# Three small attentions, each in two parts of 256 tokens and in units of 8 heads

## The reference, cut to what matters

```python
x = x + xattn0(ln(x), ctx)       # "0x": 16 heads of 16, biases
x = x + attn0(ln(x))             # "0a": keys and values from a latent of 64
x = x + moe0(ln(x))              # 32 experts, top 4, and one shared expert
x = x + xattn1(ln(x), ctx)       # keys of all 1601 context rows, one head of k and v
x = x + ln(h + attn1(h)) * gamma + beta    # "1a", h = ln(x); causal
x = x + ffn1(ln(x))              # 8 experts, the best one per token
```

## Time and profile before

| | us |
|---|---|
| median of 3 runs (lowest, highest) | 622.85 (621.93, 626.32) |
| the profiled execution | 627.66 |
| its span | 625.7 |
| 0x, 0a and the context, to `up(0)` | 0 to 143.6 |
| moe0 and xattn1 | 143.6 to 441.0 |
| 1a and the last norm, to the last gate's logits | 441.0 to 507.2 |
| the last stage | 507.2 to 625.7 |

### The profile page before, as it was taken

How to read it: one execution, slowest core, us unless ns; L and a number is a source line. 1 busy time by engine, 2 the same in 40 slices (tenths; PEclk the granted TensorE clock), 3 DMA queues, 4 the chain that set the end, 5 groups by cost and what they waited for, 6 DMA issues and landing times.

```text
span 625.7 us, 15065 instructions
## 1 busy us (share of the span) xinstructions
PE 546.8 (87%) x6480; PEld 366.6 (59%) x6480; DVE 326.8 (52%) x648; ACT 290.5 (46%) x467; POOL 111.6 (18%) x192
## 2 busy tenths in 40 slices
PE   4968758887999999789999999999797977999991
PEld 1536524553566666435677677675356544999990
DVE  2235124735566666567999989892465550011111
ACT  1434417523565666348887878787043010332220
POOL 4321141310333333350000000000300002000002
PEclk9978779998999999989999999999898888999997
DMA  8833370001455555440000000000700004388712
GB/s 321 316 129 126 138 260 1 2 15 52 130 157 154 154 151 151 158 179 3 4 3 4 2 4 4 3 3 3 270 2 2 0 2 151 117 295 288 275 35 92
DMA packets 35041, 65.01 MB, mean 104 GB/s; under 512 B 3264, under 2 KB 24640, under 8 KB 34592
## 3 DMA queue, kind: packets, MB, share of 16 engines
q1 hardware_dynamic: 31952, 59.16, 28.5%
q10 hardware_dynamic: 2640, 3.85, 1.8%
q0 software_dynamic: 384, 1.05, 0.5%
HBM read 60.05 MB, written 4.00 MB: 102 GB/s over the span
## 4 chain that ended last, share of the span: by engine, by line
PE 56%; issue 17%; DVE 11%; another core or an unknown queue 7%; DMA 4%; POOL 2%; ACT 2%; SPq 0%; POOLq 0%; ACTq 0%; DVEq 0%
PE ps L1189 9%; PE ps L1298 8%; PE ps L1266 7%; PE ps L1047 7%; PE ps L1211 7%; PE ps L1312 6%; PE ps L996 2%; DMA attn_weights<-in_wall 2%; PE ps L1092 1%; DVE region L887 1%; DVE region L765 1%; DVE region L762 1%; PE ps L1136 1%; DMA const_bf<-in_cb 1%
## 5 line engine op out<-in xcount | busy, mean ns | idle before, releaser
L887 DVE TENSOR_REDUCE region<-ps 128x1 f32<-128x512 f32 x192 | 124.1, 687 | 19.6 <-PE ps L1266 19.6
L665 ACT ACTIVATE region<-ps 128x1024 f32<-128x1024 f32 (+1 forms) x112 | 105.9, 963 | 19.7 <-PE ps L1298 19.2
L1266 PE MATMUL ps<-ctx_kT,region 96*32 96x512 bf16 x768 | 82.0, 383 | 2.6 <-DVE region L887 1.8
L1298 PE MATMUL ps<-region,ctx_kT 98*32 98x512 bf16 x832 | 72.5, 381 | 0.6 <-ACT region L643 0.4
L996 PE MATMUL ps<-const_bf 128*128 128x512 bf16 x226 | 58.5, 420 | 14.7 <-DMA const_bf<-in_cb 8.5
L1312 PE MATMUL ps<-region,ctx_v 128*32 128x128 f32 (+1 forms) x1664 | 70.1, 272 | 0.0
L1189 PE MATMUL ps<-region 128*128 128x512 f16 x264 | 63.7, 386 | 0.1
L1312 PEld LDWEIGHTS ps<-region,ctx_v 128*32 128x32 f32 (+1 forms) x1664 | 56.7, 109 | 9.5 <-issue 0.3
L694 ACT ACTIVATE region<-ps,ctx_v 128x128 f32<-128x128 f32 x88 | 25.1, 368 | 73.1 <-PE ps L1047 73.1
L438 POOL TENSOR_TENSOR region<-region 128x512 f32<-128x512 f32 x33 | 38.2, 1157 | 79.3 <-ACT region L608 77.8
L1211 PE MATMUL ps<-region 128*128 128x256 bf16 x396 | 48.6, 273 | 2.1 <-DVE region L839 2.1
(11 more groups left out here) (216 smaller groups left out, 762.8 us busy)
## 6 DMA issues: line engine op xcount, KB each, us to landing
region<-in_w SPq DMA_DIRECT2D x15, 1024.0 KB, 7.5
region<-in_ctxT SPq DMA_DIRECT2D x8, 1601.0 KB, 7.8
region<-gates SPq DMA_DIRECT2D x32, 256.0 KB, 3.4
ctx_kT<-in_w SPq DMA_DIRECT2D x7, 1024.0 KB, 7.1
region<-in_moe SPq DMA_DIRECT2D x33, 192.0 KB, 2.4
attn_weights<-in_wall SPq DMA_DIRECT2D x1, 2152.0 KB, 12.6
slots_x<-zeros SPq DMA_DIRECT2D x1, 1408.0 KB, 15.9
attn_weights<-in_wall ACTq DMA_DIRECT2D x1, 1024.0 KB, 7.4
```

The source lines that it names most:

```text
L665: act.activation(probs[u % NP_][:, 0:512 * n_keys], ps[:, pr:pr + n_keys, :].rearrange("p b n -> p (b n)"), ACT.Exp).then_inc(mq["exp"], 1)
L887: ins = dve.tensor_reduce(mp[g % 2][:, j // 3, j % 3:j % 3 + 1], bank(4 + n % 2), AX.X, ALU.max)
L1266: ins = pe.matmul(ps[32 * i:32 * i + 32, at, :], QT[0:KQ, b, h + i // 2, 32 * (i % 2):32 * (i % 2) + 32], kT[0:KQ, b, 512 * c:512 * c + 51 ...
L1298: ins = pe.matmul(ps[32 * c:32 * c + 32, 2 * (u % 2) + i, :], kT[0:KQ2, b, k * P + 32 * c:k * P + 32 * c + 32], QT[0:KQ2, b, 8 * r:8 * r + ...
```

## The change

- The 512 tokens of an attention are two parts of 256 (h = 0, 1). Norm, root, transposes, projections, bias and output of a part are instructions of their own, with semaphores per part. All of a part's data takes one bank, and each bank 0 to 3 is passed on by a written list of uses (`HEADS`): a new user waits until the last one was read.
- The softmax runs in 24 units, 8 for each attention: unit g is 8 heads of one tile (z and pT hold 512 columns and not 1024). Scores take turns in banks 4 and 5, the turned probabilities have bank 6, the values' products bank 7. ACT alone copies the turned probabilities. DVE alone writes the four k copies, two instructions for a part, each of 4 x 256 columns. ACT alone copies v.
- Each engine's queue through 0x, 0a and the context, and through 1a, is written out anew, with the second part's norm and projections between units, and `keys_turn` in two pieces (8 and 5 transposes) with one bank. Part of the context's preparation (batches 4 to 7) now stands behind 0a's softmax.
- All `keep_clock` calls of the small attentions go, with those ahead of moe0 and of the last norm. The 22 within moe0 and the 45 behind the last gate stay.
- SP issues all loads but `bcol`: k and v weights and ctx's rows first, then q and o weights, then the mask's constants; 0a's weights behind the third context batch.
- In 1a POOL adds beta to x ahead of time, and DVE makes the second norm in two instructions a tile (subtract and gamma; root and x + beta).

```diff
-        z = [r2(1024) for _ in range(2)]
-        pT = [r2(1024).rearrange("p (j q) -> p j q", j=8) for _ in range(2)]
+        z = [r2(512) for _ in range(2)]
+        pT = [r2(512).rearrange("p (j q) -> p j q", j=4) for _ in range(2)]
...
-        BANKS = {"0x": dict(xt=3, lat=7, q=5, k=3, v=(7, 5), sc=(3,), pt=5, vo=(7,), yt=3, out=(5, 6, 7, 3)),
...
+        HEADS = {
+            0: "X1a0 K1a1 O1a0 Xm11".split(),
+            1: "X1a1 Q1a1 Y1a0 Xm10".split(),
+            2: "K0x0 K0x1 X0x1 Q0x1 O0x0 Y0x1 L0a0 K0a0 L0a1 K0a1 V0a1 O0a0 Xm00 Xm01 Q1a0 V1a0 Y1a1".split(),
+            3: "X0x0 Q0x0 V0x1 V0x0 Y0x0 X0a0 O0x1 Q0a0 X0a1 V0a0 Q0a1 Y0a0 Y0a1 O0a1 K1a0 V1a1 O1a1".split(),
+        }
...
+        def unit(g):
+
+            return ("0x", "0a", "1a")[g // 8], g % 8 // 4, 2 * (g % 8 // 4) + g % 4 // 2, g % 2
...
+            sp.dma_start(wall[:, :, D:3 * D], wall_d[:, :, D:3 * D]).then_inc(wall_kv_in, 16)
+            sp.dma_start(srcT[:], a["ctx64T"].rearrange("(c p) n -> p c n", p=P)).then_inc(src_in, 16)
+            sp.dma_start(wall[:, :, 0:D], wall_d[:, :, 0:D]).then_inc(wall_qo_in, 16)
+            sp.dma_start(wall[:, :, 3 * D:4 * D], wall_d[:, :, 3 * D:4 * D]).then_inc(wall_qo_in, 16)
+            sp.dma_start(cb[:], a["cb"]).then_inc(cb_in, 16)
...
+            load_context(0)
+            sp.dma_start(brow[:], a["brow"].partition_broadcast(P)).then_inc(brow_in, 16)
+            load_context(1)
+            load_context(2)
+            sp.dma_start(wkv_l[:], a["wkvl"]).then_inc(lat_in, 16)
+            sp.dma_start(wall[:, :, 4 * D:W_TOTAL], wall_d[:, :, 4 * D:W_TOTAL]).then_inc(wall_late_in, 16)
+            sp.dma_start(gate_w[:], a["gate"].rearrange("(c p) n -> p c n", p=P)).then_inc(gate_in, 16)
+            for b in range(3, NB):
+                sp.wait_ge(kv["proj"], b - 2)
+                load_context(b)
...
+            norm_root("0x", 1)
+            norm_root("0x", 0)
...
+            add_bias("0x", 1)
+            add_bias("0x", 0)
+            split_keys(0)
+            norm_root("0a", 0)
+            add_bias("0a", 0)
+            split_keys(1)
+            add_bias("0a", 1)
+            norm_root("0a", 1)
+            split_keys(2)
+            split_keys(3)
+            norm_root("m0", 0)
+            split_keys(4)
+            norm_root("m0", 1)
+            split_keys(5)
+            split_keys(6)
+            split_keys(7)
...
+            norm_root("post", 0)
+            norm_root("m1", 0)
+            norm_root("post", 1)
+            norm_root("m1", 1)
...
+            def keys_turned(b, part):
+                lo_, n = ((0, 8), (8, 5))[part]
+                act.wait_ge(kv["keys_ps"], 2 * b + part + 1)
+                act.activation(kT[0:KQ2, b, lo_ * P:(lo_ + n) * P], ps[0:KQ2, 1, :].bitcast(BF16)[:, 0:n * P], ACT.Copy).then_inc(kv["keys"], 1)
...
+            def unit_exp(g):
+                act.wait_ge(at["z"], g + 1)
+                act.activation(z[g % 2], z[g % 2], ACT.Exp, scale=SCALE).then_inc(at["ex"], 1)
+
+            def unit_turned(g):
+                act.wait_ge(at["pt_ps"], g + 1)
+                if g >= 2:
+                    act.wait_ge(at["pv"], g - 1)
+                act.activation(pT[g % 2], bank(6).rearrange("p (j q) -> p j q", j=4), ACT.Copy).then_inc(at["pt"], 1)
...
+                    ins = dve.scalar_tensor_tensor(out=k_Tm[:, m, :, tokens(h)], in0=bc(ps[:, b, m * 256:(m + 1) * 256].unsqueeze(1), [P, 4, 256]),
+                                                   scalar=bcol[:, o:o + 1], in1=bc(vmask.unsqueeze(2), [P, 4, 256]), op0=ALU.add, op1=ALU.mult)
+                ins.then_inc(head_read[b], 1)
...
+            def unit_max(g):
+                dve.wait_ge(at["sc"], g + 1)
+                lk(dve.tensor_reduce(mx[g % 2], bank(4 + g % 2).rearrange("p (h k) -> p h k", k=T), AX.X, ALU.max))
+
+            def unit_subtract(g):
+                if g >= 2:
+                    dve.wait_ge(at["pt_ps"], g - 1)
+                dve.tensor_tensor(z[g % 2].rearrange("p (h k) -> p h k", k=T), bank(4 + g % 2).rearrange("p (h k) -> p h k", k=T),
+                                  bc(mx[g % 2].unsqueeze(2), [P, 8, T]), ALU.subtract).then_inc(at["z"], 1)
+
+            def unit_y(g):
+                n, h, t, r = unit(g)
+                o = bank(7, 136).rearrange("p (j n) -> p j n", n=34)
+                dve.wait_ge(at["pv"], g + 1)
+                lk(dve.reciprocal(rs[g % 2], o[:, :, 32:34]))
+                dve.tensor_tensor(y_sm[:, t, r * P:(r + 1) * P].rearrange("p (j x d) -> p j x d", j=4, x=2),
+                                  o[:, :, 0:32].rearrange("p j (x d) -> p j x d", x=2),
+                                  bc(rs[g % 2].unsqueeze(3), [P, 4, 2, HD]), ALU.mult).then_inc(at["y"], 1)
+
...
+            def post_centre(h):
+                dve.wait_ge(half[h]["var"], NORMS["post"])
+                for t in (2 * h, 2 * h + 1):
+                    ins = dve.scalar_tensor_tensor(out=un[:, t, :], in0=un[:, t, :], scalar=mv[:, t, 0:1],
+                                                   in1=brow[:, BR["gamma"]:BR["gamma"] + D], op0=ALU.subtract, op1=ALU.mult)
+                lk(ins)
+
+            def post_add(h):
+                dve.wait_ge(half[h]["rstd"], NORMS["post"])
+                dve.wait_ge(half[h]["beta"], 1)
+                for t in (2 * h, 2 * h + 1):
+                    ins = dve.scalar_tensor_tensor(out=x[:, t, :], in0=un[:, t, :], scalar=rstd[:, t, :],
+                                                   in1=x_beta[:, t, :], op0=ALU.mult, op1=ALU.add)
+                lk(ins)
...
+            k_out("0x", 0)
+            k_out("0x", 1)
+            unit_max(0)
+            unit_subtract(0)
+            unit_max(1)
+            unit_subtract(1)
+            unit_max(2)
+            unit_subtract(2)
+            unit_max(3)
+            unit_subtract(3)
+            unit_y(0)
+            unit_max(4)
+            unit_subtract(4)
+            unit_max(5)
+            unit_y(1)
+            unit_max(6)
+            unit_subtract(5)
+            unit_y(2)
+            unit_y(3)
+            unit_subtract(6)
+            unit_max(7)
+            unit_subtract(7)
...
+            unit_y(20)
+            o_add("1a", 0)
+            unit_y(21)
+            norm_stats("post", 0)
+            unit_y(22)
+            post_centre(0)
+            unit_y(23)
+            post_add(0)
+            norm_stats("m1", 0)
+            norm_scale("m1", 0)
+            o_add("1a", 1)
+            norm_stats("post", 1)
+            post_centre(1)
+            post_add(1)
+            norm_stats("m1", 1)
+            norm_scale("m1", 1)
             dve.wait_ge(m1["log_ps"], 1)
...
-            def turn_x(s, at, n_keep, keep_at):
-                keep_clock(n_keep, keep_at)
...
+            def unit_scores(g):
+                n, h, t, r = unit(g)
+                head_done("Q", n, h)
+                head_done("K", n, h)
+                if g >= 2:
+                    pe.wait_ge(at["z"], g - 1)
+                masked = CFG[n][0]
+                if masked:
+                    if g == 0:
+                        pe.wait_ge(cb_in, 16)
+                    pe.matmul(bank(4 + g % 2), ident_b, mask_b, start=True, stop=False, skip_group_check=True)
+                rr = slice(64 * r, 64 * r + 64)
+                for m in range(C):
+                    for b2 in range(2):
+                        q0 = (2 * t + b2) * T
+                        ins = pe.matmul(ps[64 * b2:64 * b2 + 64, 4 + g % 2, m * 256:(m + 1) * 256],
+                                        q_T[rr, m, q0:q0 + T], k_Tm[rr, m, :, q0:q0 + T],
+                                        start=not masked, stop=True, skip_group_check=True)
+                ins.then_inc(at["sc"], 1)
+
...
+            def unit_values(g):
+                n, h, t, r = unit(g)
+                pe.wait_ge(at["pt"], g + 1)
+                if g >= 1:
+                    pe.wait_ge(at["y"], g)
+                head_done("V", n, h)
...
+            k_project("0x", 0)
+            norm_turn("0x", 0)
+            q_project("0x", 0)
+            k_project("0x", 1)
+            unit_scores(0)
+            v_project("0x", 1)
+            unit_scores(1)
+            norm_turn("0x", 1)
+            v_project("0x", 0)
+            unit_turn(0)
+            unit_scores(2)
+            q_project("0x", 1)
+            unit_scores(3)
+            unit_turn(1)
+            unit_values(0)
+            unit_scores(4)
+            unit_turn(2)
+            unit_scores(5)
+            unit_values(1)
+            unit_scores(6)
+            unit_turn(3)
+            unit_values(2)
+            kv_project(0)
+            unit_values(3)
+            unit_turn(4)
+            unit_scores(7)
+            y_turn("0x", 0)
+            unit_turn(5)
+            unit_values(4)
+            kv_turn(0)
+            o_project("0x", 0)
+            unit_turn(6)
+            unit_values(5)
+            kv_project(1)
+            unit_turn(7)
```

(94 more changed lines are left out.)

809 lines of the change are left out of this document (456 added, 353 removed).

## The result

The changed kernel takes 592.89 us (median; 592.52 to 593.31), the kernel before 623.89 beside it (621.93 to 626.32): ratio 0.950, with an interval of 0.946 to 0.953. It is faster, inside the range of 567 to 603, but by 31 us in the medians where 42 were forecast. Between the two profiled executions the gain is 35.0 (spans 625.7 and 590.7), so 7 of the missing 11 are missing in the traces.

What follows compares the result with a forecast made beforehand. Queue order was taken as the bound, with PE's own work as floor. Gains of 28.4 us (first stretch) and 14 (1a) gave 42 off the median 622.85: 581; 572 to 592 at 0.60, 567 to 603 for 8 in 10.

Steps and rivals of the forecast that it cites:

- Queue heads: Rival: waits at the head of PE's queue make every softmax unit cost 3 us and not 2; 601 us; chance 0.20.
- PE cold through the softmax: Rival: short idles in the units keep PE at 1.2 GHz; 635 us at a cold share of 0.7; chance 0.06.
- The order does nothing: Rival: the context sets the first stretch's end; only the 12.6 us weights' stall and 1a's norm passes go; 603 to 622; chance 0.04.
- A finer unit adds no column on PE: Step in the first stretch's sum: splitting tiles into units leaves PE's needed work at 89.5 us, 86.8 before the last `kv_project`.
- Cold start 1.8: First stretch: the first half of 0x's k projection runs at the low clock and costs 1.8 us more.
- PE's work 86.8: First stretch: PE's needed work at the high clock before the last `kv_project` ends, 86.8 us.
- Waits 11: First stretch: PE waits 7 us by following the queues, plus 4 us of allowance for short waits not seen.
- The lower bound of the gain, 12: First stretch: gain 28.4 us, but only 12 if PE waits 24 us and not 11.
- The tail of 8.8: Between the last `kv_project` and `up(0)`: serial copies, turn, split, transposes and hand-overs for the last keys, 8.8 us.
- Nearly full PE: Rival: PE has only the listed waits and a warm clock, so 53 us go; 570 us; chance 0.10.
- POOL beside DVE: Norm scales on DVE beside POOL's splits and bias additions: 0.4 us a part, six parts, 2.4 us, inside the allowance.
- The sum of 593: By the skill's exclusion rule, ten scales and a k or x instruction could each wait 1.2 us on POOL: 593, not 581.

Runs made afterwards that it cites:

- the warm start: The changed kernel with four edits (580.79 us), plus 20 matmuls on a cleared tile ahead of the first k and 7 ahead of q: 577.49 us.
- The pairs' run: The changed kernel with the scores of a tile's two units, one on each row half, issued together into two banks: 588.00 us, ratio 0.938.
- the four edits: The changed kernel with scores in pairs, keep-alives around 1a's gaps, up(0) ahead of the last keys and the values' buffer cleared later: 580.79 us, ratio 0.930.
- the run alone: The changed kernel with only up(0) ahead of the last four key pieces, position matmuls and gate transposes ahead of up(1): 589.02 us, ratio 0.944.

## Why the prediction was right, and where it was short

**The order in the queues was the bound: right.** It was, and the change took it away. PE's waits between 8.24 and 110.3 are 4.5 us, where the forecast had 7 and 4 of allowance. *Queue heads* did not happen: no unit costs 3 us, and PE is full for 84 us on end. *PE cold through the softmax* did not either: behind the first 21 us the rows have the durations of the high clock, at a granted clock of 1.00. *The order does nothing* fell with it; its one price, the weights' stall, is 6 us and not 12.6.

**"A finer unit adds no column on PE": this is the step that failed.** It is true of columns and false of time. The forecast priced scores at 1.09 for 16 heads and the mask at 0.60: 6.8 us for 0x, 4.4 for 0a. Measured: 8 units at 1.32, and in 0a two for 1.03 and six at 1.01, 17.7 in all; 6.5 are missing. I had read x16 and 1.09 as 16 matmuls that share a price, and halved it. With one half left out, the same row stays at 1.08, so the 16 are two streams of 8 side by side; with both halves issued together again, a pair costs 1.09. The change runs them one after the other.
The Trainium skill (TensorE: Matmul & The Clock Gate, Part 3: Packing small matmuls — row/col tiling) states that matmuls on different row groups of the array run concurrently. The trace agrees, 1.08 for 8 and 1.09 for 16. It was the rule to weigh against this change, and I hadn't.

**The first stretch, term by term.** Start 7.4, measured 8.24. Cold start 1.8 (the rows' own difference is 1.71), measured 5.0: k 3.78 for 1.99, turn 1.06 for 0.60, q 3.75 for 1.97, second k 2.88 for 1.89 (the warm values are those of the warm start). PE's work 86.8, measured 97.55 less 5.0, 92.5; 6.5 more by the scores, about 0.8 less by the overlap of neighbouring rows. Waits 11, measured 4.5. Sum 107.0 against 110.3: +0.8 +3.2 +5.7 -6.5. Three terms are too low by 9.7 and one is too high by 6.5; that the sum came within 3.3 us is luck. Part of the cold start is this execution's own: the same four pieces take 11.47 in it and 8.70 to 10.32 in the profiled ones of six runs with the same start. DVE's first maximum, forecast near 19, came at 23.80 by the late and cold start; in the warm start it comes at 19.01. The lower bound of the gain, 12, does not come out of its condition either: 13 us more of waits leave 15.4, or 13.6 with both ups cold. The tail of 8.8 took 9.85, the ups 4.8 and not 5.4.

**The rest of the gain in 0x's and 0a's overlap.** A full PE means that its saved work is worth time, and work added costs it. The pairs' run shows this in part: there PE stops being full, and the next limit is close behind, the two score banks that PE and DVE hand to each other. Of the 11.6 us of PE work that it saves 4.9 arrive in the time, 3.5 by the traces. *Nearly full PE* (570) supposed the tile's price for scores; with the dearer units the 4.5 us of waits that were left in the first stretch are all that shorter waits could have given there.

**1a: 50 us forecast, 56.7 measured.** By its parts: x to the last k instruction 15.3 (the pieces named for it add up to 16.0), measured 15.6; from there to the last quotient 20.7, measured 26.3; to the scaled x 12, measured 12.8; to the logits 2, measured 2.0. The loop is what failed, and for the same cause: 2.51 us a unit on PE instead of 2.0 on DVE, which is 4 of the 5.6 for eight units. The clock in 1a was priced at 2 and 2; keep-alives around the gaps gave 4.9 in the traces, 6.7 in the time. The first maximum came 15.5 after x, the forecast had 15.4: the changed order ahead of the units was read rightly.

**POOL beside DVE.** Priced at 0.4 a part. In the trace of the changed kernel a part's scale takes 0.72 to 0.74 in six of ten, 1.10 in two, 1.68 and 2.29 in the others. A scale over 1 us was named as a sign of being wrong, and four of ten show it. The clearing on POOL's timeline:

```profile
8.23 1.91 POOL L401 MEMSET region<- 128x2176 f32 x1
```

And the scale on DVE's:

```profile
8.30 2.29 DVE L875 TENSOR_SCALAR xn<-x,ln_mean_var,ln_rstd 128x256 f32<-128x256 f32 x2 [0.28 <-POOL ln_rstd L433]
```

The scale starts 0.07 us after the clearing and ends at 10.59, 0.45 after it. The first of its two instructions took 1.98, where the median of the twenty is 0.41, and ended about 0.1 after the clearing: it stood for nearly all of it. With the clearing moved it takes 0.73, and the time stays. So the price is higher than 0.4 where it occurs, and nothing here, for PE is later.
By the Trainium skill (SBUF — State Buffer, Who interferes with whom) when such a VectorE instruction and a GpSimd one need the port pair that they share, the one issued first holds the other off for its whole length. The trace agrees at this place, 1.98 beside a clearing of 1.91. The sum of 593 that the prediction gave by this rule is the measured time by coincidence: taking away the largest of these waits moved the time by 0.1.

**Transposes and the clock.** That transposes between short units would let the clock fall, as the prediction took from the Trainium skill (TensorE: Matmul & The Clock Gate, Part 4: PE-mode transpose), is not what these runs show: turns take a quarter of PE's time in 1a's loop (0.66 of 2.51), and the granted clock stays at 1.00. Where PE was slow, it had stood: 2.08 us in the start, 3.45 and 6.57 in 1a.

**The base.** The forecast took 42 off the median, 622.85, and the execution that it summed against was 4.8 above that. The miss of 12 us in the median is made of 7.0 that the traces gained less than 42, 4.0 by which the gain of the medians (31.0) lies under that of the traces, and 1.0 by which the kernel before measured higher this time. The sum took stretches from a profiled execution that lay 4.8 above its median and subtracted their whole gain from the median; what made that execution longer is not known.

**What stays open.** Of the 3 us that the four edits lose together, 1.6 is a cold `up(0)`, and why it was cold there and not in the run alone is not shown. Nor is it tried whether 0x and 0a can have four banks. Of the change's many parts only the early weights were run by themselves, 6 of the 31 us; what halves, units and the order of the queues each bring is not separated. The profiled execution of the changed kernel reached its last `kv_project` at 108.41, three others with the same first stretch at 106.77 to 107.13. Their k, turn, q and second k took 9.78 to 10.32 for 11.47, so 1.2 to 1.7 of the +3.3 above is that execution's cold start.

## What to carry to other kernels

A row of 16 small matmuls that costs as much as 8 is not half price for 8: before a tile is split, look whether its matmuls use different rows of the array side by side, and split so that both halves stay together (by columns or heads of both halves, not one half each). Once an order fills the engine that it was meant to fill, every forecast goes by that engine's work, its cold pieces included, and each hand-over of two buffers that had been covered becomes the next bound. And an independent piece of work, here `up(0)`, belongs into the holes of a serial tail, not behind it.

## What the runs showed of the hardware

- 64-row matmuls on one half of the array: 8 take 1.08 us; 8 more on the other half, writing the other bank, take 0.01 more between them and 0.03 more behind them.
- The granted clock reads 1.00 from 8 to 16 us in the changed kernel, while a projection takes 3.78 us, and 1.99 in the warm start: at the start of a kernel this column does not show the low clock. Of the two levels, the durations speak for 1.2 GHz. In 1a it reads 0.67 from 456 to 460 us and 0.50 after, and the same projection takes 3.75 there.
- How long the start stays slow differs from execution to execution: k, turn, q and second k take 8.70 to 11.47 us in seven profiled executions with the same instructions, 6.45 in the warm start.
- 20 matmuls of 512 columns while TensorE waits for its first load, and 7 more ahead of q, gave 3.3 us of the whole. The gain was still there 90 us later, and TensorE was nearly full in between (65.2 of 70 us without them).
- A scale of 0.73 us on VectorE took 2.29 beside a clearing of 1.91 on GpSimd, which had started 0.07 us before it.
